# Moving the statistics and norm of the next block, and the final norm, within the vector engine's queue of a fused Mamba and feed-forward kernel

## What is computed

```python
x = x + layernorm(mamba(layernorm(x)))        # norms over the 256 features
x = x + layernorm(ffn(layernorm(x)))

def mamba(x):
    xi, z = x @ Wx.T, x @ Wz.T                # 512 wide
    xi = silu(causal_conv(xi, 4 taps))
    b, c = xi @ Wb.T, xi @ Wc.T               # 8 heads x 64
    dt = softplus(xi @ Wdt.T + b_dt)
    y = ssd_scan(xi, b, c, dt, -exp(log_a)) + d_param * xi
    y = normalise(y)                          # per head, over all 1024 tokens of a batch
    return (y * gn_w + gn_b) * silu(z) @ Wout.T

def ffn(x):                                   # weights binarised to alpha * sign(w)
    return gelu(x @ bw1.T + b1) @ bw2.T + b2  # 256 -> 1024 -> 256
```

## Time and profile before

| | |
|---|---|
| median of 3 runs | 1506.59 us (1506.32 to 1510.56) |
| the profiled execution | 1510.25 us, its span 1508.3 us |
| PE (TensorE matmul) busy | 1378.9 us, 91% |
| DVE (VectorE) busy | 1089.4 us, 72% |
| ACT (ScalarE) busy | 828.6 us, 55% |
| POOL (GpSimd) busy | 438.8 us, 29% |
| granted TensorE clock, mean | 0.973 |
| chain that ended last | PE 59%, issue 17%, DVE 14%, POOL 5% |

### The profile page before, as it was taken

The page is one execution under the profiler, slowest core; times in us unless marked ns, Lnnn a source line. Parts: engine busy times, 40 slices in busy tenths (PEclk is TensorE's granted clock), DMA queues, the critical chain, the costliest instruction groups (busy, mean ns, idle before and its releaser), DMA issues.

```text
span 1508.3 us, 29308 instructions
## 1 busy us (share of the span) xinstructions
PE 1378.9 (91%) x10224; PEld 928.7 (62%) x10224; DVE 1089.4 (72%) x2424; ACT 828.6 (55%) x1718; POOL 438.8 (29%) x487
## 2 busy tenths in 40 slices
PE   4898999998999989999999999999899999999776
PEld 3374757666485755757566565756547575675654
DVE  5455786858777686867959678685877769596665
ACT  3555674556745475553746557454664547555331
POOL 2020243213331332313423134322333134321343
PEclk8899999999999999999999999999999999999888
DMA  7000000101000010100001010010100000000000
GB/s 228 1 15 1 16 1 2 43 1 45 1 16 29 2 44 1 43 1 17 29 1 43 1 45 1 2 43 1 44 1 26 18 2 29 1 29 1 29 1 29
DMA packets 33352, 33.24 MB, mean 22 GB/s; under 512 B 4888, under 2 KB 31640, under 8 KB 33184
## 3 DMA queue, kind: packets, MB, share of 16 engines
q1 hardware_dynamic: 33184, 31.11, 6.3%
HBM read 22.72 MB, written 8.39 MB: 21 GB/s over the span
## 4 chain that ended last, share of the span: by engine, by line
PE 59%; issue 17%; DVE 14%; POOL 5%; ACT 2%; SPq 1%; DMA 1%; DVEq 0%; POOLq 0%; ACTq 0%
PE bank L1291 21%; PE bank L1475 7%; PE bank L1462 7%; PE bank L1412 4%; PE bank L1447 4%; PE bank L1378 4%; PE bank L1391 3%; PE bank L1369 2%; PE bank L1400 2%; PE bank L1359 1%; DVE xn L937 1%; SPq L548 1%; DVE stats_end L924 1%; PE bank L1361 1%; DVE un L937 1%
## 5 line engine op out<-in xcount | busy, mean ns | idle before, releaser
L686 POOL TENSOR_TENSOR xdw<-xdt,decays 128x512 f32<-128x512 f32 x64 | 66.7, 1043 | 432.0 <-DVE xdt L1043 431.2
L1291 PE MATMUL bank<-sh,WbT 128*128 128x512 f16 x768 | 175.2, 385 | 10.4 <-DVE sh L967 10.4
L1291 PE MATMUL bank<-sh,WcT 128*128 128x512 f16 x768 | 175.6, 379 | 0.0
L962 DVE SCALAR_TENSOR_TENSOR xs<-xi,taps,xs 128x512 f32<-128x512 f32 x192 | 152.4, 804 | 8.6 <-ACT xs L787 4.2
L1475 PE MATMUL bank<-sign2T,hh 128*128 128x256 f16 x1024 | 151.3, 275 | 2.0 <-DVE hh L1157 2.0
L881 ACT ACTIVATE yk<-bank,decays 128x64 f32<-128x64 f32 x512 | 111.7, 329 | 74.9 <-PE bank L1391 74.9
L868 ACT ACTIVATE mt<-bank 128x512 f32<-128x512 f32 x128 | 69.5, 597 | 147.3 <-PE bank L1361 147.3
L1412 PE MATMUL bank<-xdt,mt 128*128 128x64 f32 x1024 | 147.8, 266 | 0.0
L1412 PEld LDWEIGHTS bank<-xdt,mt 128*128 128x128 f32 x1024 | 134.6, 191 | 5.5
L1291 PEld LDWEIGHTS bank<-sh,WbT 128*128 128x128 f16 x768 | 73.8, 99 | 101.1 <-issue 15.3
L1462 PE MATMUL bank<-uh,sign1T 128*128 128x512 f16 x512 | 122.9, 386 | 7.5 <-DVE uh L1146 7.2
(11 more groups left out here) (182 smaller groups left out, 2717.9 us busy)
## 6 DMA issues: line engine op xcount, KB each, us to landing
xt<-L_attn_input_tensor_dram SPq DMA_DIRECT2D x16, 512.0 KB, 4.9
u<-L_attn_input_tensor_dram SPq DMA_DIRECT2D x16, 512.0 KB, 3.9
out_dram<-u SPq DMA_DIRECT2D x16, 512.0 KB, 3.0
yT<-in_L_ffn_w_dram SPq DMA_DIRECT2D x2, 1024.0 KB, 13.8
zs<-in_L_attn_Wb_dram SPq DMA_DIRECT2D x1, 1024.0 KB, 8.0
zs<-in_L_attn_Wc_dram SPq DMA_DIRECT2D x1, 1024.0 KB, 10.8
BT<-in_L_attn_Wx_dram SPq DMA_DIRECT2D x1, 512.0 KB, 4.9
BT<-in_L_attn_Wz_dram SPq DMA_DIRECT2D x1, 512.0 KB, 5.8
```

What stands on the lines that cost most here:

```text
L686: pool.tensor_tensor(xdw[n % 2][:, :, :], xdt[n % 2][:, :, :], per_head(decays[:, 1, q, :]), ALU.mult)\
L962: nc.vector.scalar_tensor_tensor(out=xs[:, c, :], in0=xi[:, c, k:k + BLK], scalar=taps[:, c, k:k + 1], in1=xs[:, c, :], op0=ALU.mult, op1= ...
L1291: mm = nc.tensor.matmul(bank(t, key)[:, :], w[i][:, k, cols(m)], v[h][:, k, :], start=(a == 0), stop=(a == len(terms) - 1))
```

## The change

In `turn_steps` the two steps `in_stat` and `in_norm` of the next block move forward: from between the chunk steps to between the products C and H. The steps `end_stat`, `end_root` and `end_norm` of the tail move back: end_stat from before `carry` 2 to behind `back` 2, end_root and end_norm from before `carry` 3 to behind `back` 3. No instruction is added or removed.

```diff
--- before.py
+++ after.py
@@ -171,18 +171,18 @@
         steps += tail(("mid_norm", j)) + own(("B", j, 1), ("decay", j)) + tail(("ff_stat", j), ("gelu_table",))
         steps += own(("B", j, 2)) + tail(("ff_norm", j)) + own(("B", j, 3))
         steps += tail(("gate", 1, 0), ("gate", 1, 1)) if j == 0 else []
+        who, nj = ("next", 0) if j else ("own", 1)
         steps += own(("C", j, 0), ("cums", j)) + tail(("uT", j)) + own(("skip", j), ("C", j, 1)) + tail(("H", j, 0), ("H", j, 1))
-        steps += own(("C", j, 2)) + tail(("H", j, 2), ("H", j, 3)) + own(("C", j, 3)) + tail(("H", j, 4), ("H", j, 5))
-        steps += own(("sums", j)) + tail(("H", j, 6), ("H", j, 7)) + own(("decays", j))
-
-        who, nj = ("next", 0) if j else ("own", 1)
+        steps += [(who, "in_stat", nj)] + own(("C", j, 2)) + tail(("H", j, 2), ("H", j, 3)) + [(who, "in_norm", nj)]
+        steps += own(("C", j, 3)) + tail(("H", j, 4), ("H", j, 5)) + own(("sums", j)) + tail(("H", j, 6), ("H", j, 7))
+        steps += own(("decays", j))
+
         both = [[("own", "back" if first else "back+O", j, m)] for m in range(2)]
         steps += own(("front", j, 0), ("front", j, 1), ("carry", j, 0)) + both[0]
-        steps += own(("front", j, 2), ("carry", j, 1)) + [(who, "in_stat", nj)] + both[1]
-        steps += own(("turn", j, 0)) + [(who, "in_norm", nj)] + own(("front", j, 3)) + [(who, "xT", nj, 0)]
-        steps += tail(("end_stat", j)) + own(("carry", j, 2), ("back", j, 2), ("turn", j, 1)) + [(who, "xT", nj, 1)]
-        steps += tail(("end_root", j), ("end_norm", j)) + own(("carry", j, 3), ("turn", j, 2), ("back", j, 3))
-        steps += own(("head_stat", j, 0)) + tail(("end_add", j))
+        steps += own(("front", j, 2), ("carry", j, 1)) + both[1] + own(("turn", j, 0), ("front", j, 3))
+        steps += [(who, "xT", nj, 0)] + own(("carry", j, 2), ("back", j, 2)) + tail(("end_stat", j)) + own(("turn", j, 1))
+        steps += [(who, "xT", nj, 1)] + own(("carry", j, 3), ("turn", j, 2), ("back", j, 3))
+        steps += tail(("end_root", j), ("end_norm", j)) + own(("head_stat", j, 0)) + tail(("end_add", j))
     return [s for s in steps if not (first and s[0] == "tail") and not (last and s[0] == "next")]
```

## The result

The changed kernel takes 1495.38 us (median of 4 runs, 1494.18 to 1495.76) against 1508.57 us for before on the same chip (4 runs, 1506.32 to 1511.05): ratio 0.9911, 95% interval 0.989 to 0.9932. The profiled execution took 1495.28 us, its span is 1493.5 us.

What follows compares the result with a forecast made beforehand. DVE's chain was taken to bound each turn through head_stat's start. Turn 0 -1.5, six loop turns +0.2, turn 7 +0.4 gave -0.9, about -1.0 us: median 1505.6 us, range 1499.5 to 1510.5.

Steps and rivals of the forecast that it cites:

- I take this gap as the price of DVE's own jump back: Between DVE's last head_stat and the next turn's yT: 2.8 to 3.3 us at all five returns, so head_stat's start sets the turn.
- The inserts among H: in_stat and in_norm enter DVE's idle gaps of 2.01 and 2.10 us before H 2 and H 4: cost 0.
- The waits in the chunks: PE's 0.50 and 0.49 us waits for chunk 2's state addition, in blocks 0 and 1, go.
- The end of DVE's turn: DVE from chunk 2's yk through end_norm: head_stat starts at 712.48 against 712.45, +0.03 us per loop turn.
- The open term: end_norm in its new place: taken as 2.19 us, ends 1.37 and 2.58, which give 1500.0 to 1508.4.
- Turn 0: in_stat no longer holds back chunk 1's yk, 0.74 us in each of two blocks: -1.5 us.
- Turn 7: Only the end_ steps move there; head_stat at 1422.40 against 1422.00: +0.4 us.
- PE then waits at gn instead: Top of a turn: PE's 1.87 us wait before xi goes, but its wait at gn grows 1 to 2 us.
- B stands 18.13 us behind yT: Top of a turn: product B still starts 18.1 us after DVE's first yT, as DVE's chain sets it.
- A: Rival: the top of a turn follows PE, not DVE; -7.9 us, 1498.7; 12%.
- B: Rival: in_norm beside POOL takes 2.58 us, making H 4 0.6 us late; +7.8 us, 1513.4; 6%.
- C: Rival: more PE idle time at gn lowers TensorE's clock, slowing z's 24 matmuls; +17.3 us, 1522.9; 3%.

Runs made afterwards that it cites:

- extra_loop: The kernel before plus four unused BN_STATS in front of the last head_stat, in the loop's turns alone: 1511.35 us, ratio 1.0011.
- all_out_before: The kernel before with turns 1 to 6 written out on PE, DVE, ACT and POOL: 1490.15 us, ratio 0.9862 to before.
- all_out_after: The changed kernel with turns 1 to 6 written out on PE, DVE, ACT and POOL: 1488.51 us, ratio 0.9857 to before.
- pad_one: The kernel before with one more DVE instruction (fulfilled waits) in turn 0, ahead of the loop: 1504.17 us, ratio 0.9955.
- after_ahead: The changed kernel with four more DVE instructions (fulfilled waits) in turn 0, ahead of the loop: 1491.64 us, ratio 0.9873 to before.

## Why the prediction was wrong

**The step that failed** is "I take this gap as the price of DVE's own jump back", and with it "2.8 to 3.3 us lie between head_stat and the next yT". The gap was DVE's return, but the price doesn't start behind DVE's last instruction. It starts at the branch, which the sequencer reaches 0.5 us before the last yk starts, and yT follows 4.8 to 5.2 us behind that start. What stands behind yk lies under it: end_norm (2.12 us), or four idle BN_STATS (extra_loop). The norm's move therefore cost nothing where I charged 2.12 us, and of the 1.5 us that the chunks gave back nothing was lost: yk of chunk 3 starts 0.9 us behind PE's last product instead of 1.63 and the return begins as much earlier. -1.51 in the chunks and -0.80 from there to yT is the -2.31 per loop turn that I forecast as +0.03.

**The rest, in the order of its steps.**
- The inserts among H at 0: right. in_norm took 1.38 us (1.37 from the earlier trace rows) and left 0.81 us.
- The waits in the chunks: gone as said, but mis-sized, 0.99 us per turn where 1.51 came. The time from the turned xn in front of the state product to that product's start fell from 1.09 (705.07 to 706.16) to 0.44 us (697.25 to 697.69): the row's idle of 0.49 us counts only from the modelled end of the matmuls before it. That is 0.65 of the 0.75 us per block; the last 0.1 lies in the state product's own 1.06 for 1.13 us and the next start.
- The end of DVE's turn: 8.28 us from yk of chunk 2 to head_stat, summed as 8.14; head_stat starts 0.1 us earlier than before, counted from B (forecast: 0.03 later). The sum was right and stood in front of the wrong price. Where nothing returns it holds to the end: 174.72 to 174.79 us, +0.07 (all_out_before, all_out_after), and turn 6, which leaves the loop, -0.12.
- The open term, end_norm in its new place: 2.19 us as taken.
- Turn 0, -1.5: the wait in front of chunk 3 is gone, and the first gn comes 2.2 us earlier, within what setup scatters. Without setup, from turn 0's first B to its gn, it is 127.54 us for 129.21, but pad_one, with the old order, has 127.41; the size stays open. Turn 7, +0.4: +0.14.
- "PE then waits at gn instead": wrong, since yT came earlier; no wait at gn. The 1.87 us in front of xi, of which I said that they go, stayed: in the changed kernel they are PE's own return (0.41 us where the loop is left, 0.33 to 0.46 where it is written out).
- B stands 18.13 us behind yT: right at all five returns. In the other kernels it is 18.0 to 19.1 us (18.78 and 18.89 at two returns of after_ahead, where the turned tile was ready but PE's xi ran partly at the low clock).

**The rivals.** A came nearest in size (1498.7) and had its premise half right: the chain moves with PE's last product, because the branch comes a fixed 0.5 us ahead of the last yk, and yk follows that product. It isn't PE that holds the top, though; it took the return on DVE for slack. The evidence that I weighed against it, 3.11 us from PE's tile to yT, was sound and excluded only that PE's tile was the limit. It did not say where the price starts. B did not come (0.81 us left at H 4), nor C (z takes 5.34 us at all five returns). No rival had a return with a fixed start. The five returns of before all had the same work behind yk, so its gaps could not tell a fixed gap from a fixed distance, but its source view could: the branch stands there 2.5 us before head_stat ends (711.3 and 713.85), so the return could not start behind head_stat. Two ends should have stood in the sum, "counted from the last instruction" and "counted from the branch"; I had only the first.

## What to carry to other kernels

A gap behind an engine's last instruction of a loop body can be what is left of the return after the work that was still queued at the branch; before moving work there, look up when the sequencer reaches the branch, and price the move both ways. Work may be free at the end of a loop body and cost time in the same place once the loop is written out: here the final norm's move, added to the in_ move, was worth -1.5 us per turn with the loop (177.83 to 176.34) and +0.9 without. If turns are few, write the loop out and tune the order then; if not, try a few dummy instructions ahead of the loop: one was worth 1.0 us per turn in before, four 0.6 in the changed kernel.
